# Third expert layer: the turn of a tile's rows moved to the front of its iteration

## The reference

```
x2 = layernorm(x).reshape(-1, 512)                  # 1024 rows
shared_out = (silu(g_s) * u_s) @ shared_w_down.T    # g_s, u_s from x2 @ shared_w_gate_up.T
probs = softmax(x2 @ gate_w.T)                      # 16 experts
topk_vals, topk_idx = top_k(probs, 2); topk_vals /= sum(topk_vals)
g, u = split(einsum('th,eih->eti', x2, w_gate_up))  # 2 x 128 columns for each expert
out_e = einsum('eti,ehi->eth', silu(g) * u, w_down) # 128 -> 512
moe_out = sum over the row's two experts of topk_val * out_e
x = x + tanh(g_ffn[2]) * (moe_out + shared_out)
```

## Time and profile before

| what | value |
|---|---|
| median of 3 runs | 2740.81 us |
| the profiled execution's own time | 2743.17 us |
| its span | 2741.4 us |
| PE busy | 2504.3 us, 91% |
| DVE busy | 1812.3 us, 66% |
| ACT busy | 1266.7 us, 46% |
| POOL busy | 1237.1 us, 45% |
| transfers | 191.68 MB, mean 70 GB/s |
| mean granted TensorE clock | 0.96 |

### The profile page before, as it was taken

How to read it: one execution, slowest core, us unless ns; L and a number is a source line. 1 busy time by engine, 2 the same in 40 slices (tenths; PEclk the granted TensorE clock), 3 DMA queues, 4 the chain that set the end, 5 groups by cost and what they waited for, 6 DMA issues and landing times.

```text
span 2741.4 us, 42172 instructions
## 1 busy us (share of the span) xinstructions
PE 2504.3 (91%) x13741; PEld 2102.1 (77%) x13741; DVE 1812.3 (66%) x3409; ACT 1266.7 (46%) x3698; POOL 1237.1 (45%) x1379
## 2 busy tenths in 40 slices
PE   4899999998889999999887888888689999999978
PEld 4788888887778888888766776665478888888854
DVE  3777777767777777777756666563377777777662
ACT  2445555454245555555524444222245555555421
POOL 4545555554244444444416556412444444444343
PEclk8999999999999999999999999899889999999989
DMA  4112222231112111111100000258601111110054
GB/s 120 48 49 97 82 94 81 101 101 62 55 66 74 35 36 39 36 35 43 58 8 16 1 1 26 85 188 298 202 23 52 36 36 39 36 35 24 26 190 161
DMA packets 67885, 191.68 MB, mean 70 GB/s; under 512 B 10097, under 2 KB 10737, under 8 KB 64730
## 3 DMA queue, kind: packets, MB, share of 16 engines
q1 hardware_dynamic: 51936, 139.85, 15.5%
q0 software_dynamic: 10224, 42.03, 4.5%
q10 hardware_dynamic: 5514, 7.11, 0.8%
HBM read 170.57 MB, written 52.14 MB: 81 GB/s over the span
## 4 chain that ended last, share of the span: by engine, by line
PE 78%; DVE 7%; issue 4%; POOL 4%; DMA 3%; ACT 3%; ACTq 0%; SPq 0%; POOLq 0%; DVEq 0%
PE B_qkv L740 31%; PE B_out L740 19%; PE B_oT L810 4%; PE B_s L790 4%; PE B_qT L780 3%; PE B_pt L800 3%; PE B_s L791 1%; PE B_s L740 1%; PE B_oT L877 1%; PE B_qT L975 1%; PE B_out L1058 1%; DVE xn L1411 1%; PE B_qkv L975 1%; POOL ring_l L2030 1%; PE B_qT L740 1%
## 5 line engine op out<-in xcount | busy, mean ns | idle before, releaser
L1241 ACT ACTIVATE W<-S,nmx 128x128 f32<-128x128 f32 x768 | 297.8, 393 | 41.4 <-DVE nmx L1509 41.4
L2038 POOL TENSOR_SCALAR rn<-ss 128x5 f32<-128x5 f32 x128 | 25.6, 200 | 617.1 <-DVE ss L1452 617.1
L1138 ACT ACTIVATE sq<-B_qkv 128x640 f32<-128x640 f32 x128 | 90.2, 705 | 420.0 <-PE B_qkv L740 420.0
L2059 POOL TENSOR_TENSOR S<-S,mask 128x512 f32<-128x512 f32 x192 | 250.9, 1307 | 20.4 <-ACT S L1079 19.1
L1527 DVE SCALAR_TENSOR_TENSOR X<-B_out,gates,X 128x512 f32<-128x512 f32 x200 | 150.3, 751 | 163.8 <-PE B_out L740 163.7
L2098 POOL TENSOR_TENSOR W<-W,rden 128x512 f32<-128x512 f32 x192 | 200.2, 1043 | 84.8 <-DVE rden L1514 84.8
L740 PE MATMUL B_qkv<-ring_h,xnT_h 128*128 128x512 f32 x544 | 217.8, 400 | 4.2 <-DVE xnT_l L1368 3.3
L740 PE MATMUL B_out<-ring_h,oT_h 128*128 128x512 f32 x516 | 207.7, 403 | 11.3 <-DVE kT L1499 6.9
L740 PE MATMUL B_qkv<-ring_l,xnT_h 128*128 128x512 f32 x544 | 216.5, 398 | 0.0
L740 PE MATMUL B_qkv<-ring_h,xnT_l 128*128 128x512 f32 x544 | 214.3, 394 | 0.0
L790 PE MATMUL B_s<-kT,qT_h 128*128 128x256 f32 x768 | 202.9, 341 | 10.6 <-DVE xnT_l L1368 9.9
(11 more groups left out here) (492 smaller groups left out, 7957.9 us busy)
## 6 DMA issues: line engine op xcount, KB each, us to landing
raw<-in_pieces SPq DMA_DIRECT2D x270, 256.0 KB, 2.7
slots_x<-in_zero SPq DMA_DIRECT2D x32, 1030.0 KB, 6.5
raw<-in_experts SPq DMA_DIRECT2D x16, 768.0 KB, 6.3
w<-in_experts SPq DMA_DIRECT2D x8, 1024.0 KB, 12.0
slots_y<-S SPq DMA_DIRECT2D x31, 256.0 KB, 5.5
sq<-slots_x ACTq DMA_DIRECT2D x8, 257.5 KB, 6.4
qk<-slots_x ACTq DMA_DIRECT2D x8, 257.5 KB, 5.5
raw<-in_ctxT SPq DMA_DIRECT2D x8, 256.0 KB, 2.7
```

The lines of the kernel that those rows point to most:

```text
L1138: act.activation(sq[:, :], B_qkv[:, 0:HG + P], ACT.Square).then_inc(*squared.now((layer, u)))
L1241: t = act.activation(W[:, k, cols(r)], S[:, k, cols(r)], ACT.Exp, bias=nmx[:, k, r:r + 1], accum_out=den[:, k, r:r + 1])
L2059: pool.tensor_tensor(S3, S3, m.unsqueeze(1).to_broadcast([P, R, P]), ALU.add).then_inc(*masked.now((layer, u)))
```

## The change

The order number of `turn2` goes from 30 to 13. In an iteration the turn of tile t now comes right behind `apply2(t)`, ahead of `turn_act2(t - 2)`, `expand2(t - 1)` and `contract2(t - 2)`. No operation is added or taken away, and no wait changes.

```
--- before.py
+++ after.py
@@ -260,7 +260,7 @@
             if t > 3:
                 self.at(first + t - 2, 10, "load_weights2" if t < E2 else "fetch_weights2", t)
             self.at(first + t, 12, "apply2", t)
-            self.at(first + t, 30, "turn2", t)
+            self.at(first + t, 13, "turn2", t)
             self.at(first + 1 + t, 20, "expand2", t)
             self.at(first + 2 + t, 15, "turn_act2", t)
             self.at(first + 2 + t, 25, "contract2", t)
```

## The result

The changed kernel takes 2754.16 us (median of 6 runs, 2750.41 to 2756.32) against 2739.83 us for the kernel before (6 runs, 2736.11 to 2744.25): a ratio of 1.0056, 95% interval 1.0045 to 1.0068, so 12 to 19 us slower. The forecast was slower, 2763, range 2749 to 2779. The profiled execution took 2754.05 us, span 2752.2 against 2741.4.

A forecast was written before the change was run, and what follows sets the result against it. The chain of tile products was taken to bound the kernel, with PE waiting on DVE's normalising and late rows. 18.5 us of chain plus 3.5 of clock made +22: 2765.2 profiled, 2763 as median; range 2749 to 2779.

The forecast's parts named there:

- The mechanism: Tiles: expand's wait for the turn's copy (17.9 us) goes, a longer wait for DVE's normalising comes; early even rows arrive late.
- The start: Up to the expand of tile 2: early turns wait for normalising and delay the expands, +3.7 us.
- The clock: Stretch of tiles: two to three half-clock drops more than now, 3.5 us; bounds none to about +18.
- The first half: Expands of tiles 3 to 13: late requests for even tiles' rows set the pace, five pairs of 10.25 us.
- The second half: Expands from tile 16 to 30: DVE's normalising sets the pace, 4.62 us a tile against 4.00, +0.62.
- DVE's side: Second half: normalising starts 0.88 or 1.51 us after the previous expand ends, behind activations and any odd result's copy.
- PE's side: Second half: from the end of normalising through both turns to the next expand 0.90 us, then expand 1.99.
- The last period: Before the expand of tile 30: no next turn stands ahead, so it is 1.0 us shorter.
- the forecast's +25: First half: by the skill's rule each of six pairs pays a clock drop, some 9 us, making the sum +25.
- The rows come in time: Rival, chance 0.22: landings under 4.9 us, engines set the pace throughout, +12.5 us, 2753.
- Faster: Rival, chance 0.04: normalising ends before the contract product, so the 17.9 us of copy waits vanish unreplaced, 2723.
- The sum: Whole chain to the expand of tile 30: 18.5 us plus 3.5 for the clock, +22, predicted 2763.

The follow-up runs named there:

- e3: Changed kernel with rows asked for early again and the normalising (A) ahead of DVE's copy of an odd result; 2740.16 us, ratio 1.0001 to the kernel before.
- e1: Changed kernel with only the rows of tile t+2 again asked for directly behind the copy of the turn; 2746.09 us, ratio 1.0018 to the kernel before.
- e5: Changed kernel with the normalising ahead of DVE's activations and copy, rows asked for ahead of ACT's copy of the turn; 2728.33 us, ratio 0.9975 to the kernel before.
- e7: e5 with the turn put back to its old order 30; 2736.99 us, ratio 1.0000 to the kernel before.

## Why the prediction was right, point by point

*The mechanism* held in both parts. The wait of E for the copy went and a longer one of the turn for A came; in the first half the rows of even tiles, asked for behind the copy of a result, set the pace. e3 gives back the whole loss in the total by moving just A and the request; its edit shortens the start as well.

*The start* was forecast at +3.7 to E(2); it was 16.80 against 11.61, +5.2. The step as told is right (T(2) behind A(2), then E(1)): E(1) came 11.25 us behind A(0) against 7.52, +3.7, where +3.5 was forecast. But E(1) fell into the half clock, 3.48 us and not 1.99, and E(2) came 5.55 behind it and not 4.31. The clock term should have held that.

*The first half* was forecast at five pairs of 10.25 us from E(3) to E(13). They took 1891.59 - 1840.46 = 51.13, 10.23 a pair. This is partly luck: the landing was 5.6 and not 5.9, from A to E it was 0.66 and not 0.90, and E lasted 1.89, which makes 9.6; the two drops of the clock added 1.3 and 1.1 us to two of the five, and what was left went in small waits. Over all of E(2) to E(15) the growth was 5.6 us, where 6.8 was forecast.

*The second half* was mis-sized. Forecast: 4.62 a tile, +0.62. Measured: 59.03 / 14 is 4.22 with the short last period; half a pair is 4.28, +0.28. The pair of 8.56 lies just above the 8.5 under which the prediction would have called itself wrong. The reading of DVE's side was right: in the earlier trace rows terms A starts at z + 0.87 and z + 1.50 (1920.06 and 1924.65, z being 1919.19 and 1923.15), against 0.88 and 1.51. Wrong was PE's side. I took 0.90 from the end of A to E from the end of the record of the turned activations; but a following product starts before that record ends. Here A ends at 1920.60 and E starts at 1921.26, 0.66 later. And E lasted 1.89 and not 1.99. The two together are 0.34 a tile, 5 us over the 15 tiles, and that is two thirds of the 8 by which 22 was too much. The last period, without a turn ahead of it, was 3.07 us, 0.9 to 1.5 less than the others, as forecast (1.0).

*The clock* was forecast at two or three drops more, 3.5 us; there were as many as before behind the start, and some 1.5 us more at E(1). Against the repeat of the kernel before it looks different: that one has no drop from E(2) to E(16) (window 1821.01 to 1883.19, clock 1.00), and both profiles of the changed kernel have two, at E(5) and E(9). Two profiles of each can't say how many drops the change adds.

Of the six late even tiles, each with 2.17 to 2.32 us of idle PE ahead of its turn, only these two went with an E at half clock (3.23 and 2.98 us). The Trainium skill, "TensorE: Matmul & The Clock Gate", section "HAM oscillation — how this bites in real kernels", shows every burst beginning slow behind a wait for a transfer, in an example whose waits are about 3 to 5 us. The waits here are shorter, so this trace does not test that example; the forecast's +25 took it over to shorter waits, and that did not come true.

*The rivals.* "The rows come in time" gave 2753, nearest to the measured 2754, and is nevertheless wrong: the rows came late (5.5 us of waits, and e1 won 10 us by asking earlier). It comes out near because its first half was too fast and its second too slow by like amounts (4.5 and 4.7 us). "Faster" was said to need another order on DVE: with that order, and the rows asked for early, e5 is 7 us faster than before, and e7 shows that it is so by the move of the turn.

*The sum.* From A(0) to E(30) the kernel grew by 13.8 us, and 22 was forecast. The start was 1.5 too low, E(2) to E(15) 1.1 too high, the part behind E(15) 5.1 too high, and the 3.5 set aside for the clock did not come on top. So 2763 against 2754 is a right mechanism with one term of its sum, PE's side of the second half, clearly too large.

## What to carry to other kernels

Moving a producer's step forward in one engine's list can do no more than move the wait, as it did here, unless what feeds it moves too: write down for each engine what stands ahead of the input of the moved step, here the normalising behind the activations on DVE and the request for rows behind a copy on ACT. A change that loses by itself can be one half of a change that wins: the turn alone +15 us, the normalising and requests alone 0, both together -7. And where an order number moves a step past the issue of a transfer, work out the loop of that buffer; asking early again won 10 us here (e1).

## What the hardware showed that I had not expected

The fp32 product that follows a transpose starts before the record of the transpose has ended: 1921.26 against 1921.15 + 0.27 = 1921.42, and it then lasts 1.89 us where behind an idle wait it lasts 1.99. Taking the end of one record for the start of the next made the chain from A to E 0.24 us too long in the forecast (0.90 against 0.66).

```profile
1921.15 0.27 PE L983 MATMUL B_s<-ident,tables 128*128 128x128 f32 x1
```

The two profiles of the kernel before differ most outside the stretch that was changed: by 10.7 us ahead of it and by 2.5 in it. They have A(0) at 1821.11 and 1810.38 us, with the same program up to there, and spans of 2741.4 and 2730.1; the granted clock of the faster is 0.968 against 0.960. An effect of some microseconds is therefore read from stretches between two fixed instructions, and the span of one execution says little on it.

```profile
core 0: 2730.1 us, clock 0.968
```
